# Expert scoring in two halves of the tokens, each followed by its expert planes, ahead of the dense layer

## The reference

```python
q = einsum('btd,ed->bte', x, W_q)                      # 4 heads, two halves each
sim = einsum('pbthn,hkpn->pbthk', q, keys)             # 2 x 64 key scores per head
sx, sy = top_k(sim, 8)                                 # per half
scores, pk = top_k(sx[..., :, None] + sy[..., None, :], 8)   # 8 of 64 pairs
de, ue = down_embed[indices], up_embed[indices]        # 4,096 experts
w = silu(einsum('btd,bthkd->bthk', x, de) * softmax(scores))
experts = einsum('bthk,bthkd->btd', w, ue)
dense = silu(x @ W_up.T) @ W_down.T                    # inner width 4,096
out = layernorm(x + dense + experts)
```

## Time and profile before

| | us |
|---|---|
| runs of the kernel before, median of 2 (lowest to highest) | 3341.03 (3329.54 to 3352.52) |
| the profiled execution | 3314.62 |
| its span on the slowest core, core 0 | 3313.1 |
| spans of the eight cores | 3298.2 to 3313.1 |
| mean granted TensorE clock of the cores | 0.713 to 0.715 |
| phase two's four chunks, from first scoring matmul to first scoring matmul | 598.2, 601.7, 598.6 |

### The profile page before, as it was taken

The page is one execution under the profiler, slowest core; times in us unless marked ns, Lnnn a source line. Parts: engine busy times, 40 slices in busy tenths (PEclk is TensorE's granted clock), DMA queues, the critical chain, the costliest instruction groups (busy, mean ns, idle before and its releaser), DMA issues.

```text
span 3313.1 us, 21346 instructions; the slowest of 8 cores (3298.2 to 3313.1 us)
## 1 busy us (share of the span) xinstructions
PE 1422.8 (43%) x6082; PEld 603.6 (18%) x6192; DVE 1234.8 (37%) x1765; ACT 729.8 (22%) x931; POOL 588.9 (18%) x270
## 2 busy tenths in 40 slices
PE   1947546200049500373980028299101747930064
PEld 0412112000014200221430013043000313410031
DVE  1643443220000767204057740503676031266602
ACT  1221221100013222211332221133222122322221
POOL 0000000000000455100035420002553000155400
PEclk9978677555569855686995558599655778965577
DMA  8101100399974300031440003044100214420012
GB/s 179 52 0 38 38 0 13 58 113 112 110 127 140 108 0 0 11 97 64 149 136 1 0 0 108 26 152 134 38 0 0 75 37 137 140 70 0 0 51 70
DMA packets 181427, 214.44 MB, mean 65 GB/s; under 512 B 24512, under 2 KB 164928, under 8 KB 180288
## 3 DMA queue, kind: packets, MB, share of 16 engines
q1 hardware_dynamic: 175776, 172.02, 17.4%
q0 software_dynamic: 5536, 41.06, 10.6%
HBM read 241.52 MB, written 46.14 MB: 87 GB/s over the span
## 4 chain that ended last, share of the span: by engine, by line
PE 34%; DVE 32%; ACT 13%; another core or an unknown queue 10%; DMA 6%; issue 4%; DVEq 1%; ACTq 0%; SPq 0%; POOLq 0%
DVE q L865 11%; DVE argc L871 8%; ACT wsil L887 7%; PE pbig L965 6%; DVE ssum L894 5%; PE pg L767 3%; PE pbig L767 3%; PE pg L798 3%; PE pbig L798 3%; DMA out<-otmp 2%; ACT big L949 2%; PE pbu L398 2%; PE ptr L939 2%; PE py L425 2%
## 5 line engine op out<-in xcount | busy, mean ns | idle before, releaser
L855 POOL TENSOR_TENSOR p<-expuv 128x1024 f32<-128x1024 bf16 x256 | 581.7, 2272 | 1918.5 <-DVE q L865 1418.5
L871 DVE TENSOR_TENSOR argc<-q,gall 128x1024 bf16<-128x1024 bf16 x256 | 255.5, 998 | 758.6 <-ACT gall L774 378.4
L920 PE MATMUL pbig<-big,ustr 128*128 128x512 bf16 x124 | 34.6, 442 | 887.8 <-DVE zf L903 887.6
L865 DVE SCALAR_TENSOR_TENSOR q<-p,thr 128x1024 bf16<-128x1024 f32 x256 | 361.8, 1413 | 44.5 <-DVE ssum L894 32.5
L887 ACT ACTIVATE wsil<-argc,rdt 128x1024 bf16<-128x1024 bf16 x192 | 220.3, 1147 | 644.2 <-DVE argc L871 644.2
L767 PE MATMUL pg<-wstr,x1b 128*128 128x512 bf16 x500 | 122.8, 399 | 361.4 <-DMA wstr<-det_b 361.0
L894 DVE TENSOR_TENSOR ssum<-ssum,wsil 128x1024 bf16<-128x1024 bf16 x192 | 175.7, 915 | 259.7 <-ACT wsil L887 259.7
L965 PE MATMUL pbig<-big,uestr 128*128 128x512 bf16 x1000 | 242.0, 397 | 33.0 <-ACT expert L975 12.0
L920 PEld LDWEIGHTS pbig<-big,ustr 128*128 128x128 bf16 x128 | 13.8, 110 | 909.0 <-issue 898.6
L982 DVE TENSOR_TENSOR zf<-zf,expert 128x512 bf16<-128x512 bf16 x32 | 11.1, 418 | 418.5 <-ACT expert L975 418.5
L774 ACT ACTIVATE gall<-pg 128x512 bf16<-128x512 f32 x64 | 38.2, 597 | 451.5 <-PE pg L767 451.5
(11 more groups left out here) (125 smaller groups left out, 1757.2 us busy)
## 6 DMA issues: line engine op xcount, KB each, us to landing
wstr<-det_b SPq DMA_DIRECT2D x32, 1024.0 KB, 5.4
wstr<-wupt_b SPq DMA_DIRECT2D x32, 1024.0 KB, 5.3
ustr<-wdnt_b SPq DMA_DIRECT2D x64, 512.0 KB, 3.7
uestr<-uem_b SPq DMA_DIRECT2D x256, 128.0 KB, 2.2
ufc_s<-u_pre SPq DMA_DIRECT2D x4, 2048.0 KB, 30.3
ufc_s<-u_own SPq DMA_DIRECT2D x4, 2048.0 KB, 11.6
det_b<-det POOLq DMA_DIRECT2D x1, 8192.0 KB, 90.1
wupt_b<-wupt POOLq DMA_DIRECT2D x1, 8192.0 KB, 166.7
```

Of the source, the lines that this page charges most:

```text
L855: return e.tensor_tensor(p1[pp][:].rearrange("p (a b) -> p a b", a=16), xb_[:, :, None].to_broadcast([128, 16, 64]), yb_[:, None, :].to_br ...
L865: return v.scalar_tensor_tensor(q2[:], p1[pp][:], thr4[:, t4 * 4 + h: t4 * 4 + h + 1], p1[pp][:], ALU.is_ge, ALU.mult)
L871: return v.tensor_tensor(argc[pp][:], q2[:], gall[:, t4 * E + ecc * 1024: t4 * E + (ecc + 1) * 1024], ALU.mult)
```

## The change

The body of the plane loop becomes a function `emit_planes(t4)`, unchanged within. The scoring loop gets an outer loop of two pairs of token groups. Each pair loads all eight blocks of `det_b` (so they are loaded twice for a chunk), scores its two token groups, and is followed by the planes of these two groups. Up and down come after both pairs, with their code unchanged. The outer and the inner loop of the transposes are exchanged (`grp` outside, `t4` inside), and behind each `grp` come the eight `uestr` loads and matmuls of the first pass that need it.

One thing is dropped: the addition (L894) of a plane is held back until the next plane has issued its `p1`, and after the last plane nothing flushes it any more. So each chunk leaves out one addition of 128 x 1024, that of the last head and last quarter of its last token group.

```diff
+                plane_it = {"it": 0, "pend": None}
+
+                def emit_planes(t4):
+                    for h in range(HEADS):
+                        for ecc in range(4):
+                            pp = plane_it["it"] % 2
+                            plane_it["it"] += 1
...
+                            if plane_it["pend"] is not None:
+                                plane_it["pend"]()
+                                plane_it["pend"] = None
...
+                                plane_it["pend"] = mk_add
+
                 gbanks = [(pg[0][:], "pg0"), (pg[1][:], "pg1"),
                           (pbig[:, 0:512], "pbig0"), (pbig[:, 512:1024], "pbig1")]
-                for ec in range(8):
-                    wb = "wstr%d" % (ec % 2)
...
-                    P.op("sync", f, reads=["det_b", wb], writes=[wb], dma=True, stream=wb)
-                    for t4 in range(4):
-                        bank, pb = gbanks[(ec * 4 + t4) % 4]
...
+                for pair in range(2):
+                    for ec in range(8):
+                        wb = "wstr%d" % (ec % 2)
...
+                        P.op("sync", f, reads=["det_b", wb], writes=[wb], dma=True, stream=wb)
+                        for tloc in range(2):
+                            t4 = 2 * pair + tloc
+                            bank, pb = gbanks[(ec * 2 + tloc) % 4]
...
+                            P.op("tensor", f, reads=[wb, "x1b"], writes=[pb])
...
+                            P.op("scalar", f, reads=[pb, "gall%d_%d" % (t4, ec)],
+                                 writes=[pb, "gall%d_%d" % (t4, ec)])
+                    emit_planes(2 * pair)
+                    emit_planes(2 * pair + 1)
 
                 for icg in range(8):          # up, then down: unchanged
...
-                it = 0
-                pend_add = None
-                for t4 in range(4):
-                    for h in range(HEADS):
-                        for ecc in range(4):
...
-                if pend_add is not None:
-                    pend_add()
-                    pend_add = None
...
-                for t4 in range(4):
-                    for grp in range(4):
+                for grp in range(4):
+                    for t4 in range(4):
                         def f(t, t4=t4, grp=grp):
...
-                for dcg in range(2):
-                    for ec in range(32):
...
+                    for ec in range(8 * grp, 8 * grp + 8):
+                        emit_eup(0, ec)
+                for dc4 in range(4):
...
+                for ec in range(32):
+                    emit_eup(1, ec)
```

More of the change, by code:

```diff
@@ L930, in build_nc, with emit_eup, f @@
                 P.op("vector", f, reads=["pbig", "x1b", "zf2"], writes=["pbig", "zf2"])
-                ss_all = ["ss%d_%d" % (t, e) for t in range(4) for e in range(4)]
-                for t4 in range(4):
-                    for grp in range(4):
+                def emit_eup(dcg, ec):
+                    ub_ = "uestr%d" % (ec % 4)
+                    uoff = (ec % 4) * 512
+                    def f(sy, dcg=dcg, ec=ec, uoff=uoff):
+                        return sy.dma_start(uestr[:, uoff:uoff + 512],
+                                            uem_b[ec * 128:(ec + 1) * 128, dcg * 512:(dcg + 1) * 512])
+                    P.op("sync", f, reads=["uem_b", ub_], writes=[ub_], dma=True, stream=ub_)
+                    def f(t, ec=ec, uoff=uoff):
+                        r = None
+                        for dc4 in range(4):
+                            r = t.matmul(pbig[:, dc4 * 512:(dc4 + 1) * 512],
+                                         uestr[:, uoff + dc4 * 128: uoff + (dc4 + 1) * 128],
+                                         big32[:, ec * CH:(ec + 1) * CH],
+                                         start=(ec == 0), stop=(ec == 31))
+                        return r
+                    P.op("tensor", f, reads=[ub_, "big32"], writes=["pbig"])
+                for grp in range(4):
+                    for t4 in range(4):
                         def f(t, t4=t4, grp=grp):
@@ new lines, in build_nc, with f @@
+                    for ec in range(8 * grp, 8 * grp + 8):
+                        emit_eup(0, ec)
+                for dc4 in range(4):
+                    def f(sc, dc4=dc4):
+                        return sc.activation(expert[:, dc4 * CH:(dc4 + 1) * CH],
+                                             pbig[:, dc4 * 512:(dc4 + 1) * 512], AF.Copy)
+                    P.op("scalar", f, reads=["pbig", "expert"], writes=["pbig", "expert"])
+                for ec in range(32):
+                    emit_eup(1, ec)
@@ L979, in f @@
+                for dc4 in range(4):
+                    def f(sc, dc4=dc4):
+                        oc = 4 + dc4
+                        return sc.activation(expert[:, oc * CH:(oc + 1) * CH],
+                                             pbig[:, dc4 * 512:(dc4 + 1) * 512], AF.Copy)
+                    P.op("scalar", f, reads=["pbig", "expert"], writes=["pbig", "expert"])
                 def f(v):
```

118 lines of the change are left out of this document (55 added, 63 removed).

## The result

The changed kernel takes 3593.6 us in the median (3578.8 to 3614.2), and the kernel before, measured beside it, 3321.3. The ratio is 1.081, with a 95% interval of 1.077 to 1.085: slower by 8.1%. Forecast were 3595 us and a ratio of 1.076. In some executions of any of these kernels the cores of a die run at a lower clock; the comparisons leave these out. The profiled execution took 3585.1 us, its span on the slowest core 3583.6, which is 270.5 more than before; the sum had 251.

A forecast was written before the change was run, and what follows sets the result against it. No engine is full: a row of stages, each with its own limit. 57.8 + 5 = 62.8 us a chunk, 251 in all, gave 3566 us profiled, 3595 on the median; 8 in 10 range 3510 to 3710.

The forecast's parts named there:

- the sum: Stage costs from first scoring matmul to L920, 57.8 us a chunk more, plus 5 for transposes: 251 us in all.
- The rival on the faster side: Up and down run under the planes if L806 is served between plane Silus: path 338 us, 3088 or 3112; 3%.
- Planes, up, down and the last load: Stages of a chunk's path: planes 132.7 us twice, up 52.5, down 58.6, block 7's load L838 7.3.
- The sum in words: Planes start 76 us earlier; second scoring 30, up 52, down with its last load 66 lie behind or between them.
- The scoring stages: First and second pair's scoring: 38.5 us (bounds 29 to 55) and 30.2 us (bounds 22 to 42).
- the ring of down: Down's two-buffer cycle of load, start and matmuls: 6.6 us for two blocks by formula, 6.7 in the trace.
- The estimate of 4.4 us for this load: A 1 MB load by the skill's 2.0 us fixed plus 436 GB/s; the trace's 5.4 was used instead.
- the rival of the falling clock: TensorE at half clock in scoring: stages 55 and 42 us, 28 us a chunk more, 3678 or 3707; 12%.
- Its argument against: In scoring, slow matmuls run without gaps, and that brought the clock back in 6 us before.
- The transposes: Expert output: three more cold starts against up to nine faster transposes; +5 us a chunk, bounds -4 and +12.
- The planes are a round trip of two engines: In the planes, DVE's addition waits for ACT 48 times, 65 us in all; round trip unchanged by the edit.
- The term of 132.7 us: Planes of two token groups, ACT's first plane to the end of plane 31, read from the earlier trace; counted twice.

The follow-up runs named there:

- e3_order: Kernel before with only the order changed: one scoring pass, all 64 planes, then up and down; all additions made. Ratio 1.072.
- e5_between: e3_order with each group of up behind one of the first 32 planes and down behind the 33rd; ratio 0.937.
- e1_outrows: Kernel before with the new expert output alone (transposes with grp outside, first-pass matmuls in four bursts); ratio 1.003.
- e8_lateadd_only: Kernel before with DVE's addition of a plane moved behind the next plane's argc, its one edit; ratio 0.993.
- e10_halfpool_late: e8_lateadd_only with POOL's product cut to half its rows (expert output not the reference's); ratio 0.931 to the kernel before.
- e9_halfpool: Kernel before with POOL's product cut to half its rows (expert output not the reference's); ratio 0.968.

## Why the prediction was right, point by point

**The direction and the mechanism.** Up and down were forecast to lie behind the planes because L806 stands behind 64 Silus in ACT's queue. e3_order shows that alone: +59 us a chunk against +57 by the same terms. The chunk periods after are 663.3, 666.9 and 667.0 us where the forecast had about 662. e5_between shows the other side: with L806 served between the Silus the path is 340.5 us. The rival on the faster side had 338, but for the split scoring, which was not run in this form; e5_between has one scoring (59.6 us to the first plane). What was right of that rival is that up and down cost nothing between the Silus, and its condition, the place in the queue, was what the change didn't have.

**The number.** That 3593.6 us was measured and 3595 forecast is luck. The forecast put its ratio on 3341 us, the median of two runs, where the kernel before has 3321.3 beside the kernel after; the ratio forecast, 1.076, lies just below the interval measured, 1.077 to 1.085. The two errors cancel.

**The terms.** Planes, up, down and the last load were within 1 us each. The price of a bubble in TensorE, a copy 3.3 and 2.7 us late at the cold start, was read rightly from the earlier trace rows. The sum in words, 76 us earlier against 30 + 52 + 66 later, makes some 73 and not 57.8; its terms hold the other 15 without saying so. 10 are the planes' two starts with two planes ready (2 x 132.7 against 275.8), and the rest is the 4.5 us from the last plane to block 7, which before stood on the path.

**The scoring stages were sized too small.** 38.5 and 30.2 against 44.2 and 33.4 in the mean, 9 us a chunk, 36 in all. The step that failed is "I take 38.5, since the ring of down shows the formula to hold". The formula holds, its inputs did not stay. The load of 5.4 us became 6.1 in the median of the kernel and 6.9 in the last chunk's first stage: from the end of a block to the start of the one that reuses its buffer it took 5.4 to 6.8 us in chunk 1 and 5.3 to 7.9 in chunk 4, where the sum had 6.0. The estimate of 4.4 us for this load by the figures of the Trainium skill (DMA: Bandwidth & Descriptors, Anatomy of one DMA) is further off still; that section gives them for DMAs that GpSimd issues, and these are SP's. And 16 matmuls did not take 3.45 us in every block. The timeline of the kernel after, blocks 2 and 4:

```profile
2967.93 6.25 PE L824 MATMUL pg<-wstr,x1b 128*128 128x512 bf16 x16 [3.63 <-DMA wstr<-det_b]
...
2982.00 6.04 PE L824 MATMUL pg<-wstr,x1b 128*128 128x512 bf16 x16 [4.36 <-DMA wstr<-det_b]
```

Behind a wait of 3.6 and 4.4 us the next 16 matmuls take 6 us again. That is the rival of the falling clock, given 12%: it did come, in part and only for blocks behind a wait, 49 and 36 us in the worst chunk where it had 55 and 42. In the four first stages 5 of the 28 blocks behind the first took 5.2 to 6.3 us, each after a wait of 2.4 to 4.4; others kept 3.6 after waits of up to 3.4. Its argument against held for one block at a time: the block behind a slow one had no wait and ran in 3.6 us. The rule of the Trainium skill named there (TensorE: Matmul & The Clock Gate, HAM oscillation) is borne out in kind by these rows, but not at every block. And 1.3 us of the first stage is the table load of ACT's first Silu, which moved here from up and which the sum left out. Of the 9 us a chunk the slow blocks make some 5 (an estimate: what they take beyond 3.6 us), the table load 1.3, and the longer loads would be the rest.

**The transposes were sized too large.** +5 us a chunk were taken; the stretch that holds them grew by 2.7, 3.1 and 1.5 us on the slowest core, by 0.7 in the mean of all, and not at all in e1_outrows, whose ratio allows 0.3% of the whole. On the slowest core the four paths came 35 us longer than summed and the rest of the kernel 15 less (4.5 us more than before, where 20 were taken), which makes the 19 us by which 251 fell short of 270.

**"The planes are a round trip of two engines" was wrong as a cause.** The term of 132.7 us did not suffer, for it was read as one piece from the earlier trace rows. But the rows of waits named the engine that came last, and behind it a longer exclusion went unseen: the earlier trace rows has 65 us of waiting for ACT, and e8_lateadd_only removes it and gains 0.7%. Whoever had costed an edit of that wait from that row would have promised 64 us a chunk and got 6.

## What to carry to other kernels

An engine's queue is in order, so moving a block of work "earlier" also moves everything else of that engine behind it: cost both the stage that starts sooner and the one that loses its cover, here 76 us and two better starts of the planes against 148. Where the moved stage leaves gaps on the engine that both need, weave the other in piece by piece; the same instructions gave 1.072 in blocks and 0.937 woven. And before an edit is costed from a wait, look whether the operation behind the wait keeps its length when the wait goes.

## What the runs showed of the hardware

POOL's product and DVE's operations with two SBUF inputs never ran at once. An `argc` of 0.69 us took 2.42 when it started 0.03 us behind POOL's, an addition of 0.69 took 2.13, a `q2` of 1.28 took 2.66, and POOL's own 1.89 became 2.41 under a DVE operation. The first of these stood in the trace of the kernel before already, 43 times:

```profile
1077.09 1.90 POOL L855 TENSOR_TENSOR p<-expuv 128x1024 f32<-128x1024 bf16 x1 [88.05 <-DVE q L865]
...
1077.12 2.42 DVE L871 TENSOR_TENSOR argc<-q,gall 128x1024 bf16<-128x1024 bf16 x1 [0.17 <-DVE q L865]
```

The Trainium skill has this (SBUF — State Buffer, Who interferes with whom): a DVE instruction with two SBUF inputs contends with a GpSimd instruction that reads SBUF, the pair of ports that they share is an exclusive lock, and the order of issue decides who blocks. The rows agree, and e10_halfpool_late shows that it costs by the sum. The time stands in the blocked operation's own length, not as a wait, so busy shares of DVE and POOL are too high by it, and no row of waits names it.

TensorE's clock had a third reading besides 1.00 and 0.50. In e1_outrows cores 2 and 3 went through the matmuls of scoring and up in chunk 3 at 0.81, 263 ns a matmul instead of 216, and cores 6 and 7 did so in chunk 4; in e9_halfpool it was cores 2 and 3 in chunk 4, while the other six had 1.00. All eight cores do this dense stretch in every chunk, and in the last chunk of the kernel before all had 0.99 or 1.00 there. What sets it off no run here shows.
